# Weight loads, row statistics and three z blocks in a new order, from the last attention heads to loop iteration 12 of a fused layer

## The chip, the cores and the metric

One core of one Trainium2 chip runs the whole layer as one program. Times are device microseconds (us) of that core, from its first to its last instruction and the little that lies around them. TensorE (PE) multiplies, VectorE (DVE) and ScalarE (ACT) are the only engines besides PE that reach PSUM, GpSimd (POOL) works in SBUF alone, and SyncE (SP) issues almost every DMA.

## The reference

Four batches of 768 tokens (256 gathered image pixels projected to 192 channels, and 512 text rows) form `h`. Then, cut to what matters:

```
h = h + normed(attention(layernorm(h))) * silu(gate) @ Wo     # 6 heads, decay mask, group norm per batch
z = layernorm(h) @ P                                          # 8 sets of 16
scores = z . C (8 sets of 64);  top 4 of 64, softmax weights w
y = sum over the 4 chosen of w * (gelu(z @ W1 + b1) @ W2 + b2)
h = h + gelu(y @ G1 + g1b) @ G2 + g2b
```

The kernel computes all 64 experts of each set and multiplies by weights that are zero where an expert isn't chosen.

## The kernel before

There are 24 tiles of 128 tokens, handled as 12 pairs (k = 0 to 11) by the attention and as 6 blocks of 512 tokens by the experts. Each engine has its own instruction list, written out by hand, and the engines meet only at semaphores, so the order inside each list is the schedule.

**Attention.** The loop over pairs does queries, keys, values and gates of pair k and the heads, masks and outputs of pair k-1. `outputs` of pair 11 stands behind the loop: PE `turn` (transposed keys), `heads` (L590), DVE `mask`, PE `outputs` (L612, L615), DVE `outputs` (L1395), `group_stats` (L1403), `gn_aggr` (L1412). The group norm of the second half of the tokens needs all six pairs 6 to 11: PE `gn_mean`, DVE `gn_dev`, PE `gn_spread`, DVE `gn_var`, ACT `gn_root`, DVE `gn_scale`. Then DVE `normed` (L1462) scales pairs 6 to 8 and ACT `normed` (L1029) pairs 9 to 11, DVE `gate_mul` (L1447) multiplies by the gates, PE `wo_pair` (L643) projects, DVE `residual` adds into `h`.

**Preparation of the experts.** `row_stats` (L1474, L1475) takes the layer norm's statistics of a pair, `variances` (seven linked instructions, L1281 to L1287) and ACT `ln_root` and DVE `shifts` finish them for a range of tiles. `x2_make` normalises a pair (ACT before the loop, POOL at L1807 inside it), PE `turn_x2` transposes it, ACT `x2_out` copies it, PE `project_z` and ACT `z_out` give z of a block, and `z_high`, `z_rest`, `z_mid`, `z_low` split it in three bf16 parts that SP stores (`store_z`). For a tile of gates: `scores`, `copy_scores` (L1074), `largest` (L1504), `mark` (L1518), `distances`, `exps`, `chosen_exps` (L1535), `normaliser`, `weights` (L1784), `turn_gates` (L670), `keep_gates` (L1094), `high_part` and `low_parts`, `store_rows` and `store_gates`.

**The main loop.** It has 24 iterations i of 8 groups n. A group is: PE four `first` matmuls (L813), ACT three gelus (L1202, L1211, L1213), PE `duo_gates` (L852), DVE two products (L1668, L1671), POOL one (L1885), PE `second` (L876) two groups later. The weights of a group come by `spread`, an SP DMA of 512 KB (L368) issued three groups ahead into four buffers `wbc`. The gates of tile i+5 are made inside iteration i. Even iterations hold the exponentials of two tiles (n = 3, with two table loads on ACT), iterations 5, 9, ... the final projection of a block. Before the change z of blocks 3, 4 and 5 is made in iterations 1, 2 and 3, and their `x2_make` runs at n = 5 and 6 of iterations 0, 1 and 2. `load_w1` issues nine DMAs (six of 256 KB at L256, three of 16 KB at L260); half 0 goes on ACT's queue between two copies of pair 11, half 1 on SP's. `keep_clock(n)` issues n dummy matmuls of 512 columns (L760).

## Time and profile before

| what | before |
|---|---|
| median of 3 runs | 905.84 us (901.13 to 906.43) |
| the profiled execution's own time | 905.14 us |
| its span, first to last instruction | 903.3 us |
| granted TensorE clock, mean | 0.986 |
| first PE matmul of the main loop (L813) | 357.70 us |
| first DVE product of the main loop (L1668) | 359.44 us |

A profile page gives busy time by engine, the chain of work that ended last, and groups of instructions by line. The timeline lists instructions in order of time with the idle time before them and what released them. The windows view gives each engine's busy time in stretches that the reader chooses; below the stretches are loop iterations, from the first L1668 of one to the first L1668 of the next.

### The profile page before, as it was taken

What the parts mean: (1) busy time and instruction counts of PE and PEld (TensorE: products, weight loads), DVE (VectorE), ACT (ScalarE), POOL (GpSimd) and SP (SyncE); (2) the same over time, 40 slices, a digit from 0 to 9 for tenths busy, and PEclk for the clock granted to TensorE, in tenths of its full rate; (3) what the DMA queues carried; (4) which work ended last, traced back from release to release, by engine and by line L of the source; (5) the groups of instructions that cost most, each with busy time, mean ns of one, the idle gap of its engine ahead of it and who ended that gap; (6) DMA issues with size and microseconds to landing.
All of it is one profiled execution on the core that took longest, in us unless ns stands there. A gap on an engine that the chain in (4) does not pass through costs nothing.

```text
span 903.3 us, 16221 instructions
## 1 busy us (share of the span) xinstructions
PE 858.9 (95%) x5414; PEld 399.1 (44%) x5414; DVE 657.6 (73%) x1608; ACT 588.4 (65%) x891; POOL 527.9 (58%) x481
## 2 busy tenths in 40 slices
PE   8799999999999989889899999999999999999997
PEld 3477777777688756222222222322232223222222
DVE  5666656665476687958688888878888887877774
ACT  2232322345442356868689898889979897988784
POOL 0456555544365624566857576758675767575552
PEclk9999999999999999899999999999999999999998
DMA  9500002000000097768588989788988888989773
GB/s 266 221 1 1 2 1 75 1 1 1 1 2 13 18 156 176 241 190 260 170 262 236 277 233 289 235 282 235 282 236 277 252 275 230 280 257 301 250 247 102
DMA packets 90110, 154.28 MB, mean 171 GB/s; under 512 B 30326, under 2 KB 56374, under 8 KB 89635
## 3 DMA queue, kind: packets, MB, share of 16 engines
q1 hardware_dynamic: 89542, 151.63, 55.6%
q10 hardware_dynamic: 486, 1.62, 1.2%
q8 instruction: 44, 0.72, 0.3%
q14 instruction: 38, 0.31, 0.1%
HBM read 138.96 MB, written 15.83 MB: 171 GB/s over the span
## 4 chain that ended last, share of the span: by engine, by line
PE 75%; ACT 10%; DVE 7%; issue 4%; POOL 2%; DMA 1%; ACTq 0%; DVEq 0%; POOLq 0%; SPq 0%
PE ps L876 17%; PE ps L813 16%; PE ps L496 5%; PE ps L852 5%; PE ps L519 3%; PE ps L590 3%; PE ps L504 3%; PE ps L643 3%; PE ps L599 3%; ACT ring L1202 2%; PE ps L529 2%; PE ps L561 2%; PE ps L581 2%; PE ps L612 2%; PE ps L664 1%
## 5 line engine op out<-in xcount | busy, mean ns | idle before, releaser
L1885 POOL TENSOR_TENSOR ring<-ring,wbc 128x512 f32<-128x512 f32 x192 | 245.0, 1278 | 151.7 <-ACT ring L1211 142.3
L1668 DVE TENSOR_TENSOR ring<-ps,ring 128x1024 f32<-128x1024 f32 x192 | 234.6, 1222 | 82.3 <-PE ps L852 55.7
L813 PE MATMUL ps<-zst,w1st 99*128 99x512 bf16 x768 | 210.9, 384 | 12.3 <-ACT ring L1202 7.3
L876 PE MATMUL ps<-ring,w2cur 128*32 128x512 f32 x1536 | 206.6, 611 | 0.0
L1202 ACT ACTIVATE ring<-ps 128x1024 f32<-128x1024 f32 x192 | 196.9, 1026 | 3.9 <-PE ps L813 3.8
L1213 ACT ACTIVATE ps<-ps 128x512 f32<-128x512 f32 x192 | 113.3, 590 | 56.5 <-PE ps L813 56.3
L1671 DVE TENSOR_TENSOR ring<-ps,wbc 128x512 f32<-128x512 f32 x192 | 130.8, 681 | 0.2 <-DMA wbc<-w_rows 0.2
L813 PEld LDWEIGHTS ps<-zst,w1st 99*128 99x128 bf16 x768 | 60.7, 97 | 137.1 <-issue 37.3
L1211 ACT ACTIVATE ring<-ps 128x512 f32<-128x512 f32 x192 | 116.6, 607 | 0.0
L1734 POOL TENSOR_TENSOR s2q<-s2q,rope 128x768 f32<-128x768 f32 x24 | 43.1, 1817 | 91.0 <-ACT s2q L1014 91.0
L852 PEld LDWEIGHTS ps<-wst,sel 32*128 32x128 bf16 x384 | 18.1, 91 | 150.7 <-DVE ring L1668 95.9
L852 PE MATMUL ps<-wst,sel 32*128 32x512 bf16 x384 | 75.0, 387 | 4.9 <-DVE ring L1668 4.7
L1725 POOL TENSOR_TENSOR t1k<-t1k,t2k 128x768 f32<-128x768 f32 x24 | 44.1, 1853 | 52.8 <-DVE t2k L1351 52.8
L994 ACT COPY zT<-ps 128x512 f32<-128x512 f32 x12 | 7.0, 586 | 94.8 <-PE ps L489 94.8
L876 PEld LDWEIGHTS ps<-ring,w2cur 128*32 128x32 f32 x1536 | 31.9, 109 | 76.3 <-issue 70.4
L496 PE MATMUL ps<-wcat,zT 128*128 128x256 f32 (+2 forms) x144 | 53.8, 511 | 6.0 <-DVE t1q L1336 4.0
L1349 DVE TENSOR_TENSOR t1k<-ps,rope 128x768 f32<-128x768 f32 x24 | 22.9, 952 | 49.7 <-PE ps L599 41.1
L1336 DVE TENSOR_TENSOR t1q<-ps,rope 128x768 f32<-128x768 f32 x24 | 23.0, 957 | 46.9 <-PE ps L529 37.9
L1784 POOL TENSOR_TENSOR wn<-mr,norm 128x512 f32<-128x512 f32 x24 | 28.0, 1165 | 39.9 <-DVE mr L1535 36.7
L1743 POOL TENSOR_TENSOR qT<-t1q,s2q 128x768 f32<-128x768 f32 x24 | 43.2, 1823 | 0.0
L1518 DVE MATCH_REPLACE8 mr<-top,sc 128x68 f32<-128x68 f32 x192 | 39.0, 213 | 0.0
L1002 ACT COPY kT<-ps 128x768 f32<-128x768 f32 x24 | 19.1, 797 | 28.5 <-PE ps L581 28.5
(181 smaller groups left out, 1297.7 us busy)
## 6 DMA issues: line engine op xcount, KB each, us to landing
wbc<-w_rows SPq DMA_DIRECT2D x192, 512.0 KB, 5.3
w2cur<-in_w SPq DMA_DIRECT2D x48, 256.0 KB, 4.9
w_parts<-wp SPq DMA_DIRECT2D x72, 64.0 KB, 3.1
zst<-z_parts SPq DMA_DIRECT2D x72, 64.0 KB, 4.3
wst<-w_parts SPq DMA_DIRECT2D x24, 128.0 KB, 4.0
z_parts<-zp SPq DMA_DIRECT2D x6, 384.0 KB, 6.3
wst<-w_parts SPq DMA_DIRECT2D x24, 96.0 KB, 3.8
out_h<-h SPq DMA_DIRECT2D x12, 192.0 KB, 5.4
```

The costliest lines, as they stand in the source:

```text
L496: pe.matmul(bank(to + a // 512, 0, w), xnT[:, k % 2, x, :], wcat[:, 0, col + a:col + a + w], start=True, stop=False)
L813: return pe.matmul(bank(to), w1st[0:99, 4 * a + j, col:col + P], zst[0:99, (i // 2) % 2, j, :], start=True, stop=True)
L852: mm = pe.matmul(bank(WBANK + j), sel[q:q + 32, n % 2, :], wst[q:q + 32, i % 2, j, :], start=True, stop=True)
L876: mm = pe.matmul(bank(YBANK, 0, 512, 32 * j, 32 * j + 32), w2cur[:, n, j, :], ring[:, (4 * g + j) % RING, :], start=False, stop=(n == 7 an ...
L1202: act.activation(ring[:, slot:slot + 2, :].rearrange("p a n -> p (a n)"), ps[:, 0:2 * BLK], ACT.Gelu_apprx_tanh).then_inc(s["duo_gelu"], 1)
L1211: act.activation(ring[:, slot + 3, :], bank(TBANK), ACT.Gelu_apprx_tanh).then_inc(s["tri_gelu"], 1)
L1213: act.activation(bank(JBANK), bank(JBANK), ACT.Gelu_apprx_tanh).then_inc(s["two_gelu"], 1)
L1668: dve.tensor_tensor(v, ps[:, WBANK * 512:WBANK * 512 + 1024], v, ALU.mult).then_inc(s["duo_done"], 1)
L1671: dve.tensor_tensor(ring[:, slot + 2, :], bank(JBANK), wbc[:, g % 4, 0, :], ALU.mult).then_inc(s["two_done"], 1)
L1725: pool.tensor_tensor(v, v, t2k[:, x, :, :].rearrange("p h d -> p (h d)"), ALU.add).then_inc(s["ak"], 1)
L1743: pool.tensor_tensor(qT[:, x, :, :].rearrange("p h n -> p (h n)"), t1q[:, x, :, :].rearrange("p h n -> p (h n)"), s2q[:, x, :, :].rearrang ...
L1885: pool.tensor_tensor(ring[:, slot, :], ring[:, slot, :], wbc[:, g % 4, 1, :], ALU.mult).then_inc(s["tri_done"], 1)
```

## The change

- **Weights.** `load_w1(0)` moves from ACT's queue to SP's, behind `store_z(0)`; `load_w1(1)` moves from before the end of attention to the last place ahead of the loop's first `spread` calls, behind `load_z(0)` and `load_gates(0)`. The first three spreads go ahead of these. The ones of `zst` are loaded in two halves. The loads of G1, g1b, G2 move into iteration 1 (semaphore `ld_final`) and that of g2b into iteration 2; `store_z(1)` and `store_z(2)` into iteration 0.
- **Statistics.** `mark(2)` and `row_stats(2)` to `(4)` go into pair 11 ahead of `rotate_keys`, `row_stats(5)` and `variances(4, 12)` to its end. `row_stats(6)` to `(9)` go to iteration 0 (n = 3), `row_stats(10)`, `(11)`, `variances(12, 24)` and `ln_root(5)` to iteration 2 (n = 3), `shifts(5)` to its n = 4.
- **Before the loop.** Heads of pair 11 ahead of `turn_gates(2)`; PE `outputs` waits for its own half's mask alone; `group_stats` by half; `chosen_exps(3)` ahead of the masks; `turn_gates(3)` ahead of the group norm; `project_z(1)` ahead of `gn_spread`; DVE `normed` in two calls (pair 6, then 7 and 8); `largest(5)` and the first part of `mark(5)` ahead of the loop. `keep_clock` goes from nine dummy matmuls to two.
- **z of blocks 3 to 5** is made in iterations 4, 8 and 12, and its `x2_make` on POOL in iterations 3, 7 and 11, one tile in each of n = 2 to 5.

```diff
+            load_w1(sp, 0)
+            store_rows(2)
+            store_rows(3)
+            store_gates(2)
+            store_gates(3)
             sp.wait_ge(s["aq"], TILES)
             sp.wait_ge(s["ak"], TILES)
-            load_w1(sp, 1)
...
+            for g in range(3):
+                spread(g)
+            sp.wait_ge(s["yg_t"], 2)
+            load_ones(0)
             sp.wait_ge(s["st_z"], 16)
             load_z(0)
+            sp.wait_ge(s["yg_t"], 4)
             sp.wait_ge(s["zeroed"], 16)
             load_gates(0)
+            load_ones(1)
+            load_w1(sp, 1)
...
-                pe.wait_ge(s["m"], 2 * k + 2)
+                pe.wait_ge(s["m"], 2 * k + x + 1)
...
+            heads(PAIRS - 1, 0)
+            heads(PAIRS - 1, 1)
             turn_gates(2, 1)
             pe.wait_ge(s["res"], 6)
-            keep_clock(2)
-            heads(PAIRS - 1, 0)
-            heads(PAIRS - 1, 1)
-            keep_clock(2)
+            keep_clock(1)
             outputs(PAIRS - 1, 0)
             outputs(PAIRS - 1, 1)
+            pe.wait_ge(s["wT_done"], 3)
+            turn_gates(3, 1)
...
-            keep_clock(2)
+            keep_clock(1)
             gn_mean(1, 6)
-            pe.wait_ge(s["x2_e"], 4)
+            project_z(1, 7)
             turn_x2(4, 2)
             gn_spread(1, 6)
             turn_x2(5, 3)
...
-                if i in (1, 2, 3):
-                    if n == 0 and i == 2:
+                if i in (4, 8, 12):
+                    later = i // 4 + 2
+                    if n == 0:
                         pe.wait_ge(s["wT_done"], tile - 1)
-                        turn_x2(2 * i + 4, PBANK)
+                        pe.wait_ge(s["s_copied"], tile + 1)
+                        turn_x2(2 * later, PBANK)
...
             keep(PAIRS - 1, 0)
-            load_w1(act, 0)
             copy_scores(3, 0)
             keep(PAIRS - 1, 1)
...
-                if g == 2:
+                if i == 0 and n == 3:
+                    for k in range(6, 10):
+                        row_stats(k)
+                if i == 2 and n == 3:
                     row_stats(10)
                     row_stats(11)
                     dve.wait_ge(s["st2"], PAIRS)
                     variances(12, 24)
...
-                if i < 3 and n in (5, 6):
-                    x2_make(2 * i + 1 + n)
+                if i in (3, 7, 11) and 2 <= n < 6:
+                    x2_make(i // 4 * 2 + 6 + (n - 2) // 2, n % 2)
```

## Rows read from the trace of the kernel before

**Rows 1.** The page's first section: engine, busy us, share of the span, instructions.

```profile
PE 858.9 (95%) x5414; PEld 399.1 (44%) x5414; DVE 657.6 (73%) x1608; ACT 588.4 (65%) x891; POOL 527.9 (58%) x481
```

**Rows 2.** Windows: iterations 0, 1, 2, 4 and 7, busy time by engine, granted clock, DMA.

```profile
359.44:389.53 30.09, 24.22 (x114) 6.34 (x115) 24.18 (x80) 23.16 (x34) 19.74 (x21) 0.83 0.67 224
389.53:413.44 23.91, 23.20 (x130) 6.62 (x129) 18.24 (x45) 19.12 (x33) 16.99 (x18) 1.00 0.79 234
413.44:443.87 30.43, 25.81 (x142) 7.55 (x141) 20.30 (x53) 24.31 (x38) 20.62 (x22) 0.94 0.69 206
...
467.72:490.15 22.43, 21.45 (x130) 5.90 (x129) 18.93 (x51) 21.43 (x31) 15.28 (x15) 1.00 0.87 259
...
535.00:554.38 19.38, 19.38 (x116) 4.98 (x115) 17.02 (x44) 16.61 (x26) 15.25 (x18) 1.00 0.83 258
```

**Rows 3.** Timeline of DVE, L1668 around the last group of iteration 2.

```profile
436.90 1.22 DVE L1668 TENSOR_TENSOR ring<-ps,ring 128x1024 f32<-128x1024 f32 x1
...
443.87 1.23 DVE L1668 TENSOR_TENSOR ring<-ps,ring 128x1024 f32<-128x1024 f32 x1 [4.54 <-PE ps L852]
```

**Rows 4.** The same, the last group of iteration 4, which ends at 490.15.

```profile
487.59 1.23 DVE L1668 TENSOR_TENSOR ring<-ps,ring 128x1024 f32<-128x1024 f32 x1
```

**Rows 5.** Timeline of ACT after pair 11; ACTq is its DMA issue.

```profile
316.80 3.15 ACTq L256 DMA_DIRECT2D w1st<-w_parts  x6
...
321.70 0.81 ACT L1002 COPY kT<-ps 128x768 f32<-128x768 f32 x1
```

**Rows 6.** The chain that ended last, 316 to 358 us: start, us, what.

```profile
322.56 2.96 PE ps L590 x24
...
341.10 6.23 PE ps L643 x36
...
349.24 6.05 PE ps L643 x36
355.29 1.72 PE ps L760 x4
```

**Rows 7.** Timeline of DVE, group norm of the second half.

```profile
332.20 1.20 DVE L1412 BATCH_NORM_AGGREGATE gmv<-gns 128x2 f32<-128x36 f32 x6
...
337.28 2.78 DVE L1462 TENSOR_SCALAR oT_b<-oT_b,gscale,gbias 128x384 f32<-128x384 f32 x6
340.09 2.69 DVE L1447 TENSOR_TENSOR oT_b<-oT_b,gate_b 128x768 f32<-128x768 f32 x3
```

**Rows 8.** Timeline of DVE, statistics in iteration 0: the first of four, the seven links' ends.

```profile
367.55 0.34 DVE L1474 BATCH_NORM_STATS2 stats<-h 128x6 f32<-128x192 f32 x1
...
368.70 1.24 DVE L1281 TENSOR_TENSOR lns<-stats 128x12 f32<-128x12 f32 x1
...
371.03 0.17 DVE L1287 SCALAR_TENSOR_TENSOR lns<-lns 128x12 f32<-128x12 f32 x1
```

**Rows 9.** Timeline of DVE, iteration 4, n = 3: the wait for the exponentials.

```profile
477.69 0.69 DVE L1535 SCALAR_TENSOR_TENSOR mr<-mr,dist 128x512 f32<-128x512 f32 x1 [1.64 <-ACT dist L1087]
```

**Rows 10.** Timeline of ACT, iteration 4, n = 3: the table load back to gelu.

```profile
477.61 1.28 ACT L1202 ACT_TABLE_LOAD   x1
```

**Rows 11.** Timeline of POOL, iteration 2, n = 6: normalising ahead of `weights`.

```profile
437.12 1.99 POOL L1807 TENSOR_SCALAR x<-h,mean,rstd 128x192 f32<-128x192 f32 x2
```

**Rows 12.** Timeline of PE, the same place.

```profile
440.26 1.09 PE L670 MATMUL ps<-ident,wn 128*128 128x128 f32 x4 [2.75 <-POOL wn L1784]
```

**Rows 13.** Timeline of SP's queue: `load_w1(1)` and the next issue.

```profile
328.49 6.02 SPq L256 DMA_DIRECT2D w1st<-w_parts  x6
...
335.61 0.36 SPq L394 DMA_DIRECT2D sel<-in_sel  x1
```

**Rows 14.** DMA, 334 to 344 us: queue, packets, MB, share; KB, us to landing.

```profile
q1 hardware_dynamic: 1125, 1.58, 106.4%
...
sel<-in_sel SPq DMA_DIRECT2D x1, 64.0 KB, 11.6
```

**Rows 15.** Windows: a stretch of iteration 0 at the low clock (columns as in rows 2).

```profile
365.00:372.00 7.00, 6.84 (x25) 1.29 (x25) 6.76 (x19) 5.48 (x8) 2.65 (x3) 0.51 0.82 277
```

More of the change, by code:

```diff
@@ L427, in _ @@
                     store_out(i // 4 - 1)
-                if n == 6 and i in (1, 2, 3):
-                    store_z(i + 2)
+                if n in (1, 2) and i == 0:
+                    store_z(n)
+                if n >= 3 and i == 1:
+                    dst, src = finals[n - 3]
+                    sp.dma_start(dst, src).then_inc(s["ld_final"], 16)
+                if n == 0 and i == 2:
+                    sp.dma_start(g2b[:, :], t["g2"][GH:GH + 1, :].to_broadcast([P, D])).then_inc(s["ld_bias"], 16)
+                if n == 6 and i in (4, 8, 12):
+                    store_z(i // 4 + 2)
                 if n == 6 and i + 1 < NIT:
@@ L785, in _ @@
             scores(4, 0)
-            keep_clock(1)
+            project_z(2, 7)
             wo_pair(6, 4)
             wo_pair(7, 5)
-            pe.wait_ge(s["x2_e"], 6)
             wo_pair(8, 2)
-            project_z(2, 7)
-            wo_pair(9, 3)
+            pe.wait_ge(s["z_e"], 3)
+            scores(LEAD, PBANK)
+            pe.wait_ge(s["wT_done"], 4)
+            wo_pair(9, 1)
             pe.wait_ge(s["res"], 7)
@@ L1451, in gate_mul, with normed @@
                     ins.then_inc(s["yg_t"], 1)
-            def normed(half):
+            def normed(k0, k1):
                 bb = 1
@@ L1567, in _ @@
                     largest(2, 0, S)
+                    mark(2, 0, S)
+                    row_stats(2)
+                    row_stats(3)
+                    row_stats(4)
                 rotate_keys(k, 0)
@@ L1614, in _ @@
                     normaliser(2)
-            for c in range(2, 6):
-                row_stats(c)
-            dve.wait_ge(s["st2"], 6)
-            variances(4, 12)
+                    row_stats(5)
+                    dve.wait_ge(s["st2"], 6)
+                    variances(4, 12)
             largest(3, 0, S)
             mark(3, 0, S)
+            chosen_exps(3)
             mask(PAIRS - 1, 0)
+            shifts(4, 4, 12)
             mask(PAIRS - 1, 1)
-            shifts(4, 4, 12)
+            normaliser(3)
             outputs(PAIRS - 1, 0)
+            group_stats(PAIRS - 1, 0)
             outputs(PAIRS - 1, 1)
-            group_stats(PAIRS - 1)
+            group_stats(PAIRS - 1, 1)
             gn_aggr(1)
-            chosen_exps(3)
-            normaliser(3)
             gn_dev(1, 6)
@@ L1638, in _ @@
             largest(4, 0, S)
+            gate_mul(9)
+            mark(4, 0, S)
             residual(6, 4)
-            gate_mul(9)
             gate_mul(10)
@@ L1644, in _ @@
             residual(8, 2)
-            mark(4, 0, S)
-            residual(9, 3)
-            row_stats(6)
+            largest(LEAD, 0, S)
+            residual(9, 1)
             residual(10, 4)
-            row_stats(7)
             residual(11, 5)
-            row_stats(8)
-            row_stats(9)
+            mark(LEAD, 0, 3)
             def finish(blk, half, at):
@@ L1683, in _ @@
                     variances(12, 24)
-                if g == 4:
+                if i == 2 and n == 4:
                     shifts(5, 12, 24)
                 if n in (0, 1) and tile < TILES:
-                    if i == 0 and n == 0:
-                        largest(tile, 0, S)
-                        mark(tile, 0, 3)
                     mark(tile, 3 * n + 3, min(S, 3 * n + 6))
```

126 lines of the change are left out of this document (56 added, 70 removed).

## The prediction

> **What bounds the kernel.** I read the page's engine list first: PE is busy 95% of the span [rows 1], so no engine off PE's path matters by its total, and what can be won are stalls and PE's own filler. Then I cut the main loop into iterations with the windows [rows 2]. The reader is to see three lengths: 22.43 us for an undisturbed even iteration (4), 19.38 for an odd one without a final projection (7), and 30.09, 23.91 and 30.43 for iterations 0, 1 and 2; iteration 3 repeats 1 with 23.85. In iteration 7 PE is busy all of the time. In an even one ACT and PE are both near 21.4 of 22.43. So the excess of the first four iterations over their undisturbed kind, 7.7 + 4.5 + 8.0 + 4.5 = 24.7 us, is what the moved work costs today. Last I read the chain between pair 11 and the loop [rows 6] with the timelines beside it.
>
> **Start of the loop, a gain of 7.7 us.** I follow PE's chain. (a) ACT issues nine weight DMAs between the first and the second copy of kT; the first six take 3.15 us, and the second copy starts at 321.70 [rows 5], after which the heads run at 322.56 [rows 6]. Without them PE's transposes of the second half set it: they end about 318.5, the copy takes 0.81, heads start near 319.4, 3.1 earlier. (b) Heads take 2.96. Each output needs its own mask alone, and the statistics of half 0 go under the outputs of half 1: another 1.1 together, so aggregation (1.20, now to 333.4 [rows 7]) ends near 329.2, 4.2 earlier. For that DVE must be free: `mark(2)` and three `row_stats` go into its wait ahead of `rotate_keys` of pair 11, which is longer than they are, and `chosen_exps(3)`, ahead of the masks, is done as the heads end. Cover gone, the latter costs 0.9 on the path. (c) `project_z(1)` ahead of `gn_spread` delays the group norm by 1.0, less 0.4 for the exponentials moved away: its scale is ready at 333.6 rather than 337.2. (d) `normed` for three pairs takes 2.78 [rows 7]; for pair 6 alone about 1.15 (a third of the elements plus the fixed part; with the second call 0.4 more in all), then one `gate_mul`, 0.9. PE could start `wo_pair(6)` at 335.7, but its own scores(4) and z of block 2 come first: 336.5, 4.6 ahead of 341.10 [rows 6]. (e) From there PE is the chain. Before: two runs of three `wo_pair` (6.23 and 6.05), 1.9 of z between, 1.72 of dummies [rows 6] and 0.86 of scores, 16.6 in all. After: 12.4 + 0.95 = 13.4. The first L813 starts at 350.0, not 357.70. DVE's list, laid out with the same durations, has the last residual at 350.5 and its first L1668 at 351.7, not 359.44. The bounds are 5 us if each of some ten semaphore hops slips by 0.3, 8.7 if the norm's wait behind `project_z` is absorbed. I take 7.7, which comes from the durations themselves.
>
> **Iteration 0, a gain of 6.3.** Out go `largest(5)` and part of `mark(5)` (counted above), statistics of two pairs, the seven `variances` links (368.70 to 371.2 [rows 8]), the sqrt tables and two `x2_make`. What is left is iteration 4's pattern, 22.4, with eight `row_stats` instructions at n = 3, 0.26 to 0.3 each (first of its kind in [rows 8]), 2.1 in sum. DVE waits 1.64 there for the exponentials [rows 9], so 0.4 stays: 22.8, 7.3 less than 30.09. The clock adds to this: a stall of the first groups behind `largest(5)` left PE short of work, and the next 7 us ran at 0.51 [rows 15]; with the cause out, I count no low stretch. Against it stands SP's queue. `load_w1(1)` is issued from about 343.8, behind the gates of tile group 0, and `spread(3)` comes behind it. Its six large issues took 6.02 [rows 13]; with the three small ones, spread 3 is issued near 350.8, its data behind 1.6 MB. Group 3 asks for it at 351.7 + 6.5 + 1.1 = 359.4. Between 334 and 344 us only 1.58 MB moved although the engines were fully busy [rows 14], so the weights take 11 us: to 355 or 356, and spread 3 lands at 358 to 360. The nearest harder row is the DMA right behind this same batch: issued at 335.61, landed 11.6 later [rows 13, 14], 18.7 after the batch began; so priced, spread 3 lands at 364.5, 5.1 late. The range is 0 to 5; that row had the other half's data still in the engines, so I take 1.0. The other SP moves (G1, G2, g2b, z stores 1 and 2) are single issues of about 0.4 in front of spreads that are three groups ahead, and their users are in iterations 4 and 5: nothing. The wait of `load_z(0)` on two gate products holds back the gates and weights alone, since the first three spreads are ahead of it.
>
> **Iterations 1, 2 and 3, gains of 4.5, 6.0 and 4.4.** Iteration 1 becomes a plain odd one, 23.91 to 19.4 [rows 2]; the finals are SP issues only. Iteration 3 becomes 19.4 from 23.85, less 0.1: its four `x2_make` halves on POOL are 1.0 each (half of 1.99 [rows 11]), beside a product of 1.28 in a group of 2.3, and `second` asks for POOL's product two groups later. Cover gone, all twelve would cost up to 12 us in three iterations; POOL is idle a fifth of an odd iteration [rows 2], so I count 0.1 here and nothing later. Iteration 2 loses z (3.6) and the stall of its last group. That group takes 443.87 - 436.90 = 6.97 [rows 3] against 490.15 - 487.59 = 2.56 in iteration 4 [rows 2, 4]: POOL spends 1.99 on `x2_make` ahead of `weights` [rows 11], PE's transposes wait 2.75 for it [rows 12], and the rest of the group queues behind. It gains 4.4. Iteration 2 also receives at n = 3 two pairs' statistics (1.1), `variances` (2.5 [rows 8], first link slow beside a POOL instruction) and on ACT the square root with one more table load, 1.28 [rows 10] + 0.2. DVE absorbs 1.64 [rows 9]; both sides leave 1.5 to 2.0, more if both contend, up to 3. I take 2.0. 30.43 - 3.6 - 4.4 + 2.0 = 24.4.
>
> **Iterations 4, 8 and 12, a loss of 10.8.** Iteration 2 of before is the same pattern at the same n, so its first seven groups price it: 436.90 - 413.44 = 23.46, against 487.59 - 467.72 = 19.87 in iteration 4 [rows 2 to 4]; 3.6 each. Bounds: 2.9, which is ACT's extra busy time (24.31 - 21.43), and 4.5, which is iteration 1's excess. POOL's new `add_bias` neighbours are in iteration 4 already.
>
> **Sum.** -7.7 - 6.3 - 4.5 - 6.0 - 4.4 + 10.8 = -18.1. Against the profiled execution, 905.14, that is 887; the median of the three runs is 905.84, near enough that I don't correct.
>
> **Rivals.** *A, the weights in front of the spreads.* The batch drains as slowly as in [rows 13, 14]; groups 3 and after wait for `wbc`, which delays 5.1 instead of 1.0: 891 to 892. For it: the full DMA engines behind that batch. Against: half of that time went to the other batch. The Trainium skill, "DMA: Bandwidth & Descriptors", section "Queues, rings and completion order", says that descriptors of one queue are consumed in ring order while different queues take turns. By that rule the stores and spreads now queue behind all of the weights on SP's ring, where ACT's queue used to alternate with them, and the time is this rival's.
> *B, the clock, on the other side.* Seven of nine dummies are gone. If PE falls to the lower level, 1.2 GHz, at its first wait after the heads (near 324) and stays there up to the loop, its 22 us of work from heads to the last `wo_pair` take up to as much again: the loop starts at 372, and the sum turns to +4: 909. It decides against the change once more than 18 us of PE work runs at half speed. For it: PE did run at 0.51 after a stall [rows 15], and iteration 2, with its wait of 2.75 [rows 12], shows a mean of 0.94 [rows 2]. Against: my layout has no PE wait above 1.2 us ahead of the loop, and the first matmul of the loop is reached with PE busy nearly all of the last 14 us. The same skill, "TensorE: Matmul & The Clock Gate", section "HAM oscillation", ties such drops to recurring idle gaps; by the gaps that I find it would not act here.
> *C, the norm's chain keeps its length.* The heads gain 3.1, but the order of DVE and ACT lists (exponentials ahead of masks, two table loads, x2 copies ahead of `gn_root`) returns what (b) to (d) win: start gain 3.1 only, 891.7. For it: seven engine changes in a row there. Against: each list has idle time at that point.
>
> **Chances.** Forecast 0.58 (883 to 890), A 0.20 (890 to 895), C 0.10, better than 883 with z cheaper in the even iterations 0.05, B with its partial forms 0.07. The range of 881 to 896 takes in the bounds of the start (5 to 8.7), of z (8.7 to 13.5 for the three) and of the weights (0 to 5), and leaves out B. Within 1% (about what a measurement of this kernel can tell from no change) means above 896.8: faster 0.88, same 0.08, slower 0.04, the last when B and A meet.
>
> **What would show it.** In the changed profile: first L1668 at 351 to 353; iterations 0 to 3 of 23 to 24, 19.4, 24.4 and 19.5; 4, 8 and 12 of 26, and 16 and later unchanged. A shows as DVE or POOL waiting on wbc at groups 3 to 6. B shows as a granted clock near 0.5 between 324 and 352. C shows as heads near 319.4 with the first L813 after 353. I am wrong if PE's stalls simply reappear in the even iterations at n = 3 to 5, where ACT is full.

## The result, and the profile after

| what | before | after |
|---|---|---|
| median (13 runs each, same chip) | 905.43 us | 896.94 us (893.08 to 901.68) |
| ratio after / before, 95% interval | | 0.9908 [0.989, 0.9927] |
| the profiled execution's own time | 905.14 us | 900.31 us |
| last xnT copy of the attention loop (pair 11) | 285.49 | 288.07 |
| from there to the first product of the loop | 73.95 | 75.57 |
| first to last product of the loop | 531.54 | 522.61 |

The change gains 8.5 us, not 18. The marks in this table are starts in the two traces. The xnT copy is ACT's copy of the normalised tokens at the head of a pair (L994 in before; the rows name its tile zT). The profiled execution of after is 2.58 us late before the changed code begins: pair 11's xnT copy comes at 288.07 instead of 285.49, and pair 1's was already as late (44.24 instead of 41.66) in code that both kernels share. In all these executions pair 1's copy stands between 39.59 and 44.28, in the same code, so kernels are compared here from pair 11's copy on: 73.95 + 531.54 = 605.49 before, 75.57 + 522.61 = 598.18 after, 7.3 less. In the rows of after L820 is the kernel before's L813, L859 its L852, L883 its L876, L1679 and L1682 its L1668 and L1671, L1897 its L1885, L655 its L643, L602 its L590.

The page's first section of after, to be read against [rows 1]:

```profile
PE 854.4 (95%) x5400; PEld 398.0 (44%) x5400; DVE 657.9 (73%) x1614; ACT 589.0 (66%) x891; POOL 527.8 (59%) x481
```

Nothing in the totals tells the difference, as nothing in them told what could be won. Windows of after, iterations 0 to 4 and 7 (columns as in [rows 2]: length, PE, PEld, DVE, ACT, POOL, granted clock, DMA share, GB/s):

```profile
363.64:387.61 23.97, 23.97 (x115) 6.59 (x115) 21.01 (x57) 22.09 (x32) 14.95 (x15) 0.78 0.98 270
387.61:408.02 20.41, 19.50 (x117) 4.98 (x116) 17.11 (x43) 16.65 (x27) 13.91 (x16) 1.00 0.90 256
408.02:433.34 25.32, 22.82 (x130) 5.99 (x129) 21.42 (x64) 23.03 (x33) 15.05 (x16) 0.93 0.82 241
433.34:452.71 19.37, 19.37 (x117) 5.08 (x116) 17.01 (x43) 16.61 (x26) 19.05 (x23) 1.00 0.89 253
452.71:478.71 26.00, 24.13 (x142) 7.33 (x141) 20.30 (x52) 24.23 (x38) 15.67 (x16) 1.00 0.80 243
523.57:542.94 19.37, 19.37 (x117) 5.08 (x116) 17.01 (x43) 16.61 (x26) 19.11 (x23) 1.00 0.88 277
```

The loop did nearly what was forecast. Iterations 0 to 3 fell by 6.1, 3.5, 5.1 and 4.5; 4, 8 and 12 rose from 22.43 to 26.0 each. The DMA share of iteration 0 is 0.98 where it was 0.67: the first sign of what follows. PE is busy in all of iteration 0, at a mean granted clock of 0.78; that comes back below. Now the stretch that answers to [rows 6]. The timeline of PE, after:

```profile
322.05 2.94 PE L602 MATMUL ps<-qT,kT 128*128 128x128 f32 x24 [0.89 <-ACT kT L1009]
...
340.49 2.22 PE L655 MATMUL ps<-wo,oT_b 128*128 128x192 f32 x12
344.33 4.17 PE L655 MATMUL ps<-wo,oT_b 128*128 128x192 f32 x24 [1.62 <-DVE oT_b L1456]
...
349.19 6.27 PE L655 MATMUL ps<-wo,oT_b 128*128 128x192 f32 x36
361.54 1.01 PE L820 MATMUL ps<-zst,w1st 99*128 99x512 bf16 x2 [6.07 <-DMA zst<-in_ones]
```

PE's own work ahead of the loop ends near 355.4, 67.4 after the last copy; before it ended at 357.0, 71.5 after the copy. Then PE stands for 6.07 us until a DMA of 12 KB has landed, and the gain of the start is gone. SP's queue shows what stood around that DMA (start, duration of the issues, line, count):

```profile
321.01 2.92 SPq L256 DMA_DIRECT2D w1st<-w_parts  x6
...
333.01 10.89 SPq L327 DMA_DIRECT2D w_parts<-wp  x6
...
346.29 1.87 SPq L368 DMA_DIRECT2D wbc<-w_rows  x3
348.20 0.47 SPq L386 DMA_DIRECT2D zst<-in_ones  x1
348.78 3.80 SPq L338 DMA_DIRECT2D zst<-z_parts  x6
...
354.04 0.30 SPq L386 DMA_DIRECT2D zst<-in_ones  x1
354.39 3.85 SPq L256 DMA_DIRECT2D w1st<-w_parts  x6
...
359.21 7.01 SPq L368 DMA_DIRECT2D wbc<-w_rows  x2
```

Ahead of the ones stand the first three spreads (1.5 MB), behind them the second half of w1 (1.6 MB, here called the batch). Windows of after and then of before, 10 us each, show the DMA engines (last two columns):

```profile
340.00:350.00 10.00, 8.38 (x45) 7.12 (x44) 9.89 (x38) 6.10 (x12) 7.71 (x9) 1.00 0.44 128
350.00:360.00 10.00, 5.44 (x33) 4.88 (x31) 6.62 (x25) 1.01 (x2) 1.52 (x2) 1.00 1.03 241
360.00:370.00 10.00, 8.46 (x23) 1.98 (x23) 6.22 (x16) 6.63 (x10) 4.82 (x5) 0.53 1.05 163
370.00:380.00 10.00, 10.00 (x51) 2.37 (x51) 7.76 (x20) 9.52 (x13) 4.10 (x5) 0.79 1.05 333
```

```profile
330.00:340.00 10.00, 8.25 (x41) 4.30 (x38) 8.63 (x31) 4.79 (x12) 1.04 (x1) 1.00 1.06 171
340.00:350.00 10.00, 9.87 (x48) 7.39 (x47) 9.16 (x20) 6.37 (x15) 5.99 (x7) 1.00 0.75 152
350.00:360.00 10.00, 9.69 (x48) 6.64 (x46) 6.23 (x30) 4.72 (x8) 3.35 (x5) 1.00 0.64 190
360.00:370.00 10.00, 6.65 (x25) 1.63 (x28) 9.81 (x39) 7.26 (x11) 6.21 (x6) 0.76 0.90 308
370.00:380.00 10.00, 9.78 (x57) 2.46 (x49) 8.70 (x24) 9.93 (x15) 4.14 (x4) 0.90 0.59 185
```

After, the engines are at their limit from 350 to 380, just where PE needs its first data; before, they had been full from 330 to 340, while PE needed nothing, and had room in each of the next four windows. A share of 1.05 with only 163 GB/s (360 to 370, while the batch moves) and the same share with 333 GB/s (370 to 380, the spreads) say that a byte of the batch is about twice as dear.

### The profile page after: what moved, and what is told of

Read it like the earlier page. It is cut to its first block, busy times and chain, and to the rows that moved or that the text cites. A ratio compares the mean times of both kernels' runs of the same rounds, so it can differ in the third digit from the quotient of the medians.

```text
span 898.5 us, 16202 instructions
## 1 busy us (share of the span) xinstructions
PE 854.4 (95%) x5400; PEld 398.0 (44%) x5400; DVE 657.9 (73%) x1614; ACT 589.0 (66%) x891; POOL 527.8 (59%) x481
## 4 chain that ended last, share of the span: by engine, by line
PE 79%; ACT 10%; DVE 6%; issue 2%; DMA 2%; POOL 0%; SPq 0%; DVEq 0%; POOLq 0%; ACTq 0%
PE ps L883 18%; PE ps L820 18%; PE ps L508 6%; PE ps L859 6%; PE ps L531 3%; PE ps L516 3%; PE ps L602 3%; PE ps L611 3%; PE ps L541 2%; PE ps L593 2%; ACT ring L1210 2%; PE ps L573 2%; PE ps L624 2%; PE ps L655 1%; PE ps L676 1%
## 5 line engine op out<-in xcount | busy, mean ns | idle before, releaser
L1897 POOL TENSOR_TENSOR ring<-ring,wbc 128x512 f32<-128x512 f32 x192 | 245.1, 1278 | 151.0 <-ACT ring L1219 142.5
L1679 DVE TENSOR_TENSOR ring<-ps,ring 128x1024 f32<-128x1024 f32 x192 | 234.7, 1222 | 79.9 <-PE ps L859 51.5
L820 PE MATMUL ps<-zst,w1st 99*128 99x512 bf16 x768 | 212.9, 388 | 20.6 <-ACT ring L1210 10.7
L883 PE MATMUL ps<-ring,w2cur 128*32 128x512 f32 x1536 | 205.5, 608 | 0.0
L1682 DVE TENSOR_TENSOR ring<-ps,wbc 128x512 f32<-128x512 f32 x192 | 130.9, 682 | 1.4 <-DMA wbc<-w_rows 1.3
L820 PEld LDWEIGHTS ps<-zst,w1st 99*128 99x128 bf16 x768 | 61.3, 98 | 141.9 <-issue 42.9
L859 PEld LDWEIGHTS ps<-wst,sel 32*128 32x128 bf16 x384 | 18.1, 91 | 149.3 <-DVE ring L1679 92.7
L859 PE MATMUL ps<-wst,sel 32*128 32x512 bf16 x384 | 75.6, 390 | 1.5 <-DVE ring L1679 1.3
L883 PEld LDWEIGHTS ps<-ring,w2cur 128*32 128x32 f32 x1536 | 31.7, 108 | 77.4 <-issue 69.8
L508 PE MATMUL ps<-wcat,zT 128*128 128x256 f32 (+2 forms) x144 | 55.9, 528 | 4.9 <-DVE t1q L1345 2.9
```

The lines of the kernel that those rows point to most:

```text
L508: pe.matmul(bank(to + a // 512, 0, w), xnT[:, k % 2, x, :], wcat[:, 0, col + a:col + a + w], start=True, stop=False)
L820: return pe.matmul(bank(to), w1st[0:99, 4 * a + j, col:col + P], zst[0:99, (i // 2) % 2, j, :], start=True, stop=True)
L859: mm = pe.matmul(bank(WBANK + j), sel[q:q + 32, n % 2, :], wst[q:q + 32, i % 2, j, :], start=True, stop=True)
L883: mm = pe.matmul(bank(YBANK, 0, 512, 32 * j, 32 * j + 32), w2cur[:, n, j, :], ring[:, (4 * g + j) % RING, :], start=False, stop=(n == 7 an ...
L1679: dve.tensor_tensor(v, ps[:, WBANK * 512:WBANK * 512 + 1024], v, ALU.mult).then_inc(s["duo_done"], 1)
L1682: dve.tensor_tensor(ring[:, slot + 2, :], bank(JBANK), wbc[:, g % 4, 0, :], ALU.mult).then_inc(s["two_done"], 1)
```

## The experiments

All ratios are to the kernel before on the same chip. "Start" is the time from the last xnT copy to the first product of the loop, "loop" from first to last product. All eighteen kernels are told, in the order of the questions.

**1. The wait for the ones (e1, e2, e3).** My first reading was that a shared semaphore makes PE wait for ones that only group 16 needs.

```diff
-t["ones"][:, 1024 * m:1024 * m + 1024]).then_inc(s["ld_late"], 16)
+t["ones"][:, 1024 * m:1024 * m + 1024]).then_inc(s["ld_ones1" if m else "ld_late"], 16)
-            pe.wait_ge(s["ld_late"], 16 * 3)
+            pe.wait_ge(s["ld_late"], 16 * 2)
+                    pe.wait_ge(s["ld_ones1"], 16)
```

> The changed kernel, with the second half of the ones counted on a semaphore of its own and awaited at group 16, its first user, and not ahead of group 0. Theory 1 (the wait for this small load is what holds the start of the loop): PE idles under 1 us instead of 6.07 between the last wo_pair and the first L820-type matmul, the stretch at the low clock behind it is gone or shorter, and the ratio to the kernel before is 0.983 to 0.985, 5 to 7 us better than the changed kernel. Rival (the first z parts or gates land as late, and the wait only changes its name): the idle time stays above 4 us and the ratio stays at 0.990.

Measured: 897.71 us, 0.9905 [0.987, 0.994], start 74.08, loop 527.04. The wait changed its name (timeline of PE, e1):

```profile
359.42 0.59 PE L820 MATMUL ps<-zst,w1st 99*128 99x512 bf16 x2 [3.93 <-DMA zst<-z_parts]
361.45 0.61 PE L860 MATMUL ps<-wst,sel 32*128 32x512 bf16 x2 [1.44 <-DMA wst<-w_parts]
```

The z parts and the gates are just as late. That theory fell: the ones, the z parts and the gates are all late. The next kernel sends the batch into the loop, one of its nine pieces behind each spread of groups 3 to 11; e3 has both edits.

```diff
-            load_w1(sp, 1)
+                if 3 <= g < 12:
+                    load_w1(sp, 1, (g - 3,))
```

> The changed kernel, with the nine loads of weight half 1 issued one per group in groups 3 to 11 instead of in one batch ahead of the loop; the wait for the ones stays. Theory 1 (the ones land 7.1 us after their issue because 1.6 MB of weights share the DMA engines behind them): they land within 3 us, PE idles 1.5 to 2.5 us, ratio 0.984 to 0.987. Rival (they land late because of what is in front of them, z parts and gates): landing stays above 6 us and the ratio near 0.990. Spreads of groups 4 to 12 have one more issue in front of each; if DMA is the limit there, DVE waits on wbc in iterations 0 and 1, 1 to 2 us.

> Both edits together. If the semaphore alone removes the wait (theory 1 of the first run), this adds only what the weights cost the first spreads: 0 to 1.5 us more, ratio 0.981 to 0.985. If the spreads were late behind the weights (rival A of the prediction), the first four groups get 3 to 5 us shorter than in the first run, ratio below 0.981.

Measured: e2 903.64 us, 0.9976 [0.9955, 0.9996], start 72.68, loop 529.90; e3 904.43 us, 0.9984 [0.9963, 1.0006], start 71.83, loop 529.84. Against after, the start gains 2.9 and 3.7, and the loop loses 7: iteration 1 takes 27.48 us in e2, with DVE waiting for `wbc` in five groups (up to 3.2). None of the expected ratios came: the loop had been expected to pay 2 us at most. The work went to another place and was paid there.

**2. The loop's part alone (e4).** The kernel before with z of blocks 3 to 5 in iterations 4, 8 and 12 and `x2_make` in 3, 7 and 11, nothing else.

```diff
-                if i in (1, 2, 3):
+                if i in (4, 8, 12):
-                if i < 3 and n in (5, 6):
-                    x2_make(2 * i + 1 + n)
+                if i in (3, 7, 11) and 2 <= n < 6:
+                    x2_make(i // 4 * 2 + 6 + (n - 2) // 2, n % 2)
```

> The kernel before with one part of the change alone: z of blocks 3 to 5 in iterations 4, 8 and 12, its x2_make on POOL in 3, 7 and 11. By the prediction's sum: iteration 0 gains 3.8 (no x2_make ahead of the gates), 1 gains 4.5, 2 gains 8.0, 3 gains 4.4, and 4, 8 and 12 lose 3.6 each: 9.9 us, ratio 0.989. Rival (the stalls come back in the even iterations, which have no room): under 4 us, ratio above 0.995.

Measured: 896.21 us, 0.9902 [0.9865, 0.9939], start 73.95, loop 525.45. The forecast for this part held (0.989), and it is worth as much as the whole change, within the intervals. Iterations 0 to 4 take 26.29, 23.04, 23.30, 19.38 and 26.01; iteration 0 lost the stall of its last group, iteration 1 has one wait for `wbc` of 3.06. So all that was done ahead of the loop and to the statistics returns nothing, net, within the intervals: in the traces after's loop is 2.8 shorter than e4's and its start 1.6 longer.

**3. The batch elsewhere on the queue (e5 to e8).** The diff is e5's. In e6 and e7 the batch stands right behind `load_w1(sp, 0)`, e7 with e1's edit besides; e8 leaves the batch and puts half 0 back on ACT's queue.

```diff
             store_gates(2)
+            load_w1(sp, 1)
             store_gates(3)
...
-            load_w1(sp, 1)
```

> The changed kernel with one move undone: weight half 1 is issued behind the gates of tile 2, about where it stood in the kernel before, not in front of the loop; half 0 stays on SP's queue. Theory 1 (the 1.6 MB of weight half 1, slow to drain, was hidden ahead of the loop and now stands in its way): the ones and z parts land within 4 us, PE idles under 2 us ahead of the loop instead of 6.07, landing of spreads in the first 50 us of the loop falls from 7 to 8 us to near 5, no waits on wbc; 6 to 8 us better than the changed kernel, ratio 0.982 to 0.985. Rival (DMA work before the loop is the same in any order, so the start is as late): ratio 0.988 to 0.991.

> The changed kernel with both weight halves back to back on SP's queue as soon as attention's weights are free, ahead of the rows and gates of tiles 2 and 3. Theory 1: the DMA engines are full from 321 to 343 and free afterwards, the loop starts earliest of all orders, ratio 0.980 to 0.985. Rival: the stores of gates 2 land after 343, POOL's high part of tile 3 and with it the gates of block 0 come late, and PE waits for wst as long as it waits now: ratio 0.988 or more.

> As the run before, and the second half of the ones on its own semaphore. If the ones land quickly once the weights are out of the way (theory 1), this changes nothing beyond 1 us. If they are slow by themselves, it gains 2 to 4 us over the run before.

> The changed kernel with the other move undone: weight half 0 is issued on ACT's queue again, half 1 stays in front of the loop. By the prediction (part a) the heads of pair 11 start 3 us later, and so does what follows, ratio 0.993 to 0.994 against 0.991 of the changed kernel. If DMA sets the start of the loop (theory 1), the 3 us are hidden behind its wait of 6.07 and the ratio stays at 0.990 to 0.992.

Measured: e5 899.48 us, 0.9934 [0.9908, 0.9959], start 78.18, loop 521.16. e6 908.23 us, 1.0028 [1.0009, 1.0046], start 87.78. e7 908.72 us, 1.0019 [0.9995, 1.0044], start 86.56. e8 896.10 us, 0.9883 [0.9851, 0.9916], start 74.34, loop 521.72. The loop is clean in e5 as its theory said (iterations 1 and 2 take 19.38 and 23.98), the start is not. With nothing of w1 behind the ones, e5 has PE waiting for them still longer than after, 8.66 us; so "the weights behind the ones" fell too as the whole cause: what stands *in front* holds them. In e5 that is the spreads and, as part 4 shows, the batch, by way of a store. e6 is what its rival said, and e7 adds nothing clear of the intervals to it. In e6 both halves are in front of the small stores of gates 2, and POOL, which may not overwrite their buffer, stands (timeline of POOL, e6):

```profile
349.69 0.40 POOL L1802 CAST wp<-wT_even 128x256 bf16<-128x256 f32 x1 [21.50 <-DMA w_parts<-wp]
```

In after the same wait is 6.72, and in e8, with half 0 on ACT's queue, 3.65. That is the rule of the Trainium skill, "DMA: Bandwidth & Descriptors", section "Queues, rings and completion order": a queue's descriptors go in its ring's order, while queues take turns. The three waits agree with it. The total came out the same in e8 as in after, within the intervals, as the second expectation had it. The heads of pair 11 start 37.16 after the xnT copy instead of 33.98, so the 3.2 us of part (a) of the prediction are real on PE's list, and yet the start is 1.2 earlier: PE's list did not set it.

**4. Who goes first (e9, e10, e11).** In e9 the first three spreads go behind the gates and ones, the batch stays last. e10 also has the batch behind the store of gates 2; e11 besides has half 0 on ACT's queue.

```diff
-            for g in range(3):
-                spread(g)
             sp.wait_ge(s["yg_t"], 2)
...
             load_ones(1)
+            for g in range(3):
+                spread(g)
             load_w1(sp, 1)
```

> The changed kernel with the first three spreads issued behind the z parts, the gates of block 0 and the ones, as in the kernel before, and weight half 1 still last. Theory 2 (1.5 MB of spreads in front of 0.6 MB that PE needs first hold the loop): the ones land within 3 us, PE idles under 2 us instead of 6.07, the first product of the loop stands 4 to 5 us earlier, measured from the last xnT copy; spread 0 is now awaited by group 0, 0 to 2 us. Iterations 1 and 2 still pay 2.4 us for weight half 1. Ratio 0.985 to 0.988. Rival (the DMA engines are full up to 362 whatever the order): the start stays and the ratio stays at 0.990.

> As the run before, and weight half 1 issued behind the gates of tile 2. If both orders matter, the loop is clean from iteration 1 (19.4 and 24.0, seen with this place of the weights) and the start is no later than in the run before: ratio 0.981 to 0.985. If the batch pushes the gates' stores and z parts back by its 11 us, as it seems to have done with the spreads in front, the start is 2 to 4 us later than in the run before and the ratio 0.986 to 0.990.

> As the run before, with weight half 0 back on ACT's queue. The rows and gates of tiles 2 and 3 are no longer behind it on SP's ring, POOL's wait for the store of gates 2 falls from 6.7 to under 4, but the heads of pair 11 are 3 us later. If DMA sets the start, ratio equal to or up to 2 us below the run before. If PE's chain does, 2 to 3 us above it.

Measured: e9 898.23 us, 0.9933 [0.9909, 0.9958], start 68.87, loop 529.27. e10 893.03 us, 0.9872 [0.9845, 0.9898], start 72.83, loop 521.25. e11 896.23 us, 0.9893 [0.9865, 0.9921], start 76.02, loop 522.19. In e9 PE waits for no DMA at all, and for the first time its own chain is seen bare: 68.87, a gain of 5.1 on before. It is all given back in iteration 0, which takes 32.98 (timeline of DVE, e9):

```profile
373.01 0.69 DVE L1682 TENSOR_TENSOR ring<-ps,wbc 128x512 f32<-128x512 f32 x1 [10.42 <-DMA wbc<-w_rows]
```

The fourth group's weights stand behind the batch, and the expected ratio of 0.985 to 0.988 did not come. e10 has the lowest median of the kernels with all the work in them, 4 us under after's (3.3 by the ratios, whose intervals just meet); it came as its second expectation said. The batch in front, where the engines were half idle, costs PE 3.74 us for the ones and nothing that shows in iterations 0 and 1 (23.5 and 19.37).

How it costs that is seen on SP's queue. `load_gates(0)` waits until `store_gates(3)` has landed, and in e10 this store stands behind the batch. Its last piece (issue view, e10) and the gates' load (queue) are:

```profile
w_parts<-wp SPq DMA_DIRECT2D x1, 64.0 KB, 11.8
...
352.42 0.34 SPq L349 DMA_DIRECT2D wst<-w_parts  x1
```

The same two in e9, with all three pieces of the store:

```profile
w_parts<-wp SPq DMA_DIRECT2D x3, 64.0 KB, 1.7
...
346.48 0.36 SPq L349 DMA_DIRECT2D wst<-w_parts  x1
```

So the load of the gates goes out 67.2 us after the xnT copy in e10 and 61.0 in e9, and the second half of the ones goes out behind it. e11, whose order of batch, small loads and spreads is nearly that of before, has the same wait: POOL's wait falls to 3.83 as expected, but its gates go out at 70.3, PE waits 3.01 for the ones, and the start is the latest of the three. In e5 the gates go out at 66.4, in after at 64.6.

**5. Less at a time, and a shorter chain (e12, e13, e14).** e12 is after with `normed(6, 8)` in one call. e13 is e9 with four pieces of the batch behind the store of gates 2 and five behind that of gates 3, and nothing of it behind the spreads; e14 is both. (Where the expectations say blocks 0 to 2 and pairs 6 and 7, the edits move the spreads of groups 0 to 2 and norm pairs 6 to 8.)

```diff
+            load_w1(sp, 1, range(4))
             store_gates(3)
+            load_w1(sp, 1, range(4, 9))
```

> The changed kernel with DVE's normed for pairs 6 to 8 in one call, as before (undoes one part of step d). In the changed kernel the two calls take 1.63 + 3.09 us, against 2.78 in one call before, and PE waits 1.62 for the second gate product. If splitting costs (fixed parts, and POOL's high part beside it), one call takes 2.8 to 3.5 and the last wo_pair ends up to 1 us earlier. As PE waits 6.07 for DMA behind it, the time doesn't change in either case: ratio 0.990 to 0.992.

> The changed kernel with the spreads of blocks 0 to 2 behind the gates of block 0 and the vector of ones, and with the second half of w1 in two parts: four pieces behind the store of gates 2, five behind the store of gates 3. Theory (the DMA engines' time ahead of the loop is the limit, and with the spreads behind the small loads the engines stood idle in two stretches of 10 us, 330 to 350): the pieces of the first part fall into the idle stretches and those of the second are half a batch only, so PE waits under 2 us for the ones or z parts, the first product of the loop comes 69 to 71 us after the last xnT copy, the loop takes 521 to 523 us, and the ratio to the kernel before is 0.982 to 0.986 (about 890 us). Rival (anything of w1 ahead of the small loads holds them by the same latency): PE still waits 3.5 us or more, start at 72 to 73, ratio 0.987.

> As e13_w1_split, and the oT of pairs 6 and 7 are normed in one call instead of two. Theory: with PE's own chain setting the start, the shorter chain of VectorE shows as 1 us less than e13_w1_split, ratio 0.981 to 0.985. Rival (the DMAs still set the start): no difference from e13_w1_split, since the wait grows by what the chain gains.

Measured: e12 896.48 us, 0.9901 [0.9868, 0.9935], start 74.51, PE's wait 5.75. e13 895.39 us, 0.9899 [0.9872, 0.9926], start 74.5, loop 520.85, PE's wait 5.18. e14 896.99 us, 0.9919 [0.989, 0.9949], start 75.48, PE's wait 7.1. My theory of e13 missed: the DMA engines are then full without a break from 320 to 360 (shares 1.08, 0.97, 1.09, 0.95 in its 10-us windows), the idle stretches are filled, and there is still not enough time. In e12 and e14 PE's last `wo_pair` ends 0.75 and 1.2 us earlier after the xnT copy than in after and e13. The start does not follow it: 1.1 earlier in e12, 1.0 later in e14. So e14's rival held in the main, and one start that hangs on a DMA is known to about 1 us; three starts of before's order (before, e4, e18) lie within 0.13.

**6. The batch alone, moved and left out (e15 to e18).** e15 is the kernel before with nothing changed but the batch's place: behind the first three spreads, as in after.

```diff
-            load_w1(sp, 1)
...
             for g in range(3):
                 spread(g)
+            load_w1(sp, 1)
```

> The kernel before with the second half of w1 alone moved, to just behind the first three spreads ahead of the loop. Theory (the batch takes some 11 us of all DMA engines, and costs nothing in the kernel before only because it drains in a stretch in which the engines are idle): the loop's first spreads land late, iterations 0 and 1 grow by 5 to 10 us together, ratio to the kernel before 1.005 to 1.011. Rival (the batch isn't what the changed kernel waits for): ratio 0.998 to 1.002.

Measured: 910.91 us, 1.0078 [1.0051, 1.0105], start 74.18, loop 538.59. Iteration 0 takes 36.59 instead of 30.09, and the waits of 357 to 395 us in e15 hold two that before has none of there:

```profile
POOL ring L1885 <- DMA wbc<-w_rows: 13.8, 1, 13.8
...
DVE ring L1671 <- DMA wbc<-w_rows: 8.9, 1, 8.9
```

So the late batch costs 5.4 us by the medians (910.91 against 905.52; 6.5 in iteration 0), in an order that is otherwise the old one. The last three leave the batch's six large pieces out; the slots of the second half are computed with the first half's weights, with the same instructions.

```diff
             for n, k in enumerate((0, 1, 0, 2, 0, 1)):
+                if a:
+                    continue
-w1st[0:99, 4 * a + j, col:col + P]
+w1st[0:99, j, col:col + P]
```

> The changed kernel with the six large pieces of the second half of w1 (1.5 MB) left out, nothing else moved; the slots of the second half are computed with the weights of the first, so the output differs in those columns, and the instructions of all engines are the same. Theory (the batch's 11 us of DMA time are what the start and the late spreads cost): PE waits under 2.5 us for the ones or z parts instead of 6.07, the first product of the loop comes 69 to 72 us after the last xnT copy instead of 75.57, the loop takes 520.5 to 521.5 instead of 522.61, ratio to the kernel before 0.981 to 0.986. Rival (PE's own chain or the clock sets the start): start 74 or later, ratio 0.988 to 0.991.

> As e16_no_w1b, with the first three spreads behind the gates of block 0 and the vector of ones (the edit of e9_spreads_behind_gates). Theory: start at 68.9 as in e9_spreads_behind_gates, and iteration 0 without its gap of 16.15 us: 22.5 to 23.5, loop 520.5 to 521.5, ratio 0.980 to 0.983, the predicted 887 or near it. Rival: the spreads are late in any case, since they are issued where they are needed: iteration 0 above 26, ratio 0.985 or more.

> The kernel before with the same six pieces left out. Theory (there the batch drains in a stretch in which the engines would be idle): nothing to gain, ratio 0.998 to 1.001. Rival (the batch costs the kernel before as much as the changed one, so that it can't be what separates them): ratio 0.990 to 0.995.

Measured: e16 894.94 us, 0.9885 [0.9864, 0.9907], start 73.84, loop 521.33. e17 893.90 us, 0.9858 [0.9831, 0.9886], start 68.93, loop 522.54. e18 905.88 us, 1.0004 [0.9991, 1.0017], start 73.83, loop 531.44. The kernel before pays nothing for the batch, under 0.1% by the interval. Windows of e18, to be read against the same two of before above:

```profile
330.00:340.00 10.00, 8.25 (x41) 4.30 (x37) 8.66 (x31) 4.81 (x12) 1.04 (x1) 1.00 0.51 131
340.00:350.00 10.00, 9.87 (x48) 7.38 (x47) 9.16 (x20) 6.37 (x15) 6.01 (x7) 1.00 0.17 35
```

The shares fall by 0.55 and 0.58, so the batch is 11.3 us of all DMA engines, and before it lay in time that nobody else wanted. e16's theory missed: without the batch the start gains 1.7 only, because the three spreads in front still hold the ones. Its numbers are near those of the rival, but what PE waits for is a DMA and not its own chain (timeline of PE, e16):

```profile
355.30 1.01 PE L822 MATMUL ps<-zst,w1st 99*128 99x512 bf16 x2 [4.28 <-DMA zst<-in_ones]
```

e17 moves these too, and the wait is gone (timeline of PE, e17):

```profile
349.25 6.27 PE L657 MATMUL ps<-wo,oT_b 128*128 128x192 f32 x36
355.36 0.60 PE L822 MATMUL ps<-zst,w1st 99*128 99x512 bf16 x2
```

Start 68.93 and iteration 0 at 23.72 stand together only here. e17's start came as expected; its ratio did not (0.980 to 0.983 was expected), nor did its loop. So moving the spreads behind the small loads gives 6.7 us of the start with the batch there (75.57 - 68.87, e9) and 4.9 without it (73.84 - 68.93, e17 against e16), and leaving out the batch alone gives 1.7. And the batch takes 9.3 of iteration 0 once the start is early (32.98 in e9, 23.72 in e17). In every order tried with all the work in it, one of the two came late.

## Why the prediction was wrong

The direction was right, but the size falls just short of "faster by over 1%", which was given 0.88: the ratio is 0.991, and "same" had been given 0.08. The time missed the range of 881 to 896 by 0.9 us. From the last xnT copy on, the forecast was 18.1 less and 7.3 came: 10.8 short.

**The step that failed is "Start of the loop, a gain of 7.7 us".** The start came out 1.6 us later than before, 9.3 short. The runs split this in two, each part known to about 1 us.

- *Part (e), "From there PE is the chain": 6.6 us short, shown by e9 and e17.* I laid out PE's, DVE's and ACT's lists and never SP's: not when the ones, z parts and gates would land, only when the spreads would. The three moved spreads were costed as nothing because their own users aren't hurt; but the small loads behind them are. In before the gates went out at 353.1 to 354.0 with the spreads behind, and landed in 2.0 to 2.2 us; in after they took 4.4, 5.9 and 7.6. For the batch I had "the weights take 11 us" from [rows 14], which is right (11.3), and didn't ask what else needs the engines in the same 40 us.
- *The same gap, in the term for spread 3.* The batch was to be issued at 343.8 and spread 3 to land at 358 to 360. Less the offset of 2.58, the batch went out at 351.8 and POOL had spread 3 at 369.8, 10 us behind the 359.4 at which the forecast asks for it; the range was 0 to 5. In e9, where the start is early, this is the wait of 10.42. In after it hides behind the late start (timeline of POOL, after):

```profile
372.37 1.28 POOL L1897 TENSOR_TENSOR ring<-ring,wbc 128x512 f32<-128x512 f32 x1 [2.21 <-DMA wbc<-w_rows]
```

  The harder price in the prediction, 364.5, doesn't follow from its rows either: 350.8 + 11.6 and 343.8 + 18.7 are 362.4 and 362.5, 3 us late and not 5.1.
- *Parts (b) to (d): 2.7 us too much, seen in e9 and e17 (68.87 and 68.93; 66.25 was forecast).* Allowing for the offset of 2.58, the heads stand at 322.05 where 322.0 was forecast, so part (a) is right to 0.1, and e8, which undoes it, has them 3.2 later. Aggregation ends at 333.05, 1.25 late; the group norm's scale stands at 337.65, 1.45 late; the first `wo_pair` at 340.49, 1.4 late. The second stands another 1.62 for `oT_b`. The timeline of DVE, after:

```profile
326.04 0.69 DVE L1543 SCALAR_TENSOR_TENSOR mr<-mr,dist 128x512 f32<-128x512 f32 x1 [0.56 <-ACT dist L1085]
326.65 0.95 DVE L1396 TENSOR_TENSOR pT<-ps,causal 128x768 f32<-128x768 f32 x1
...
331.85 1.20 DVE L1421 BATCH_NORM_AGGREGATE gmv<-gns 128x2 f32<-128x36 f32 x6
...
337.65 1.63 DVE L1470 TENSOR_SCALAR oT_b<-oT_b,gscale,gbias 128x128 f32<-128x128 f32 x6
339.31 0.96 DVE L1456 TENSOR_TENSOR oT_b<-oT_b,gate_b 128x768 f32<-128x768 f32 x1
340.19 3.09 DVE L1470 TENSOR_SCALAR oT_b<-oT_b,gscale,gbias 128x256 f32<-128x256 f32 x6
```

  The mask starts 1.7 after the heads' end (324.99) because `chosen_exps(3)` sits in front of it and its exponentials end late; the cover that I named for it isn't there. And `normed` in two calls is 1.63 + 3.09 = 4.7 against 2.78 in one [rows 7]; I had counted 1.15 for the first and 0.4 for the split. The second call is that long because POOL works beside it; in e6, where POOL stands for its store until 349.69, it isn't (timeline of DVE, e6):

```profile
335.78 2.02 DVE L1470 TENSOR_SCALAR oT_b<-oT_b,gscale,gbias 128x256 f32<-128x256 f32 x6
```

  In after POOL is there because it waited 6.72 for the store behind w1's half 0, and came into DVE's way at 339.31. e7, where POOL stands as well, has 2.02 too. e12 takes the split back, and PE's last `wo_pair` ends 0.75 earlier.

**The rest of the sum held, in part by luck.** Iteration 0: 23.8 forecast, 23.97 measured, out of two terms that were wrong. The 1.0 for the late spreads cost nothing that shows, since the late start hid them. "I count no low stretch" was wrong: PE ran at 0.50 behind the wait (windows of after, under the rivals) and was busy in all of the iteration, where the pattern taken from iteration 4 has PE busy 21.45 of 22.43. Iteration 0 of e13 and of e6 (windows) shows it with the DMA engines a quarter idle: PE is again busy in all of it, and the length goes with the granted clock.

```profile
360.01:384.60 24.59, 24.59 (x115) 6.67 (x115) 21.05 (x57) 22.18 (x32) 14.97 (x15) 0.76 0.73 220
371.43:394.62 23.19, 23.19 (x115) 6.51 (x115) 21.05 (x58) 21.93 (x32) 14.95 (x15) 0.81 0.76 231
```

Iteration 1: 19.4, measured 20.41; the late weights reach it, with DVE waiting 0.94 for `wbc` at 406.81. It is 19.4 in e5, e8, e10, e13, e16 and e17, but in e12 too, which has after's DMA order, so this 1.0 doesn't come in every execution. Iteration 2: 24.4, measured 25.32. In the kernels with the changed statistics it takes 24.0, or 25.3 and more, and the granted clock tells which: 1.00 in the six with 24.0 (e3, e5, e8, e9, e12, e13), 0.93 or less in all others. The group at n = 3 takes 7.25 in each of them; the two groups behind it are longer where the clock fell. Iteration 2 of e9 (windows), to be read against after's above:

```profile
406.66:430.63 23.97, 21.45 (x130) 5.92 (x129) 21.43 (x63) 22.97 (x33) 13.79 (x14) 1.00 0.87 262
```

So iteration 2 held but for 1.4 us of clock, and why the clock falls there in one kernel's trace and not in another's stays open. Iteration 3: 19.5, measured 19.37. Iterations 4, 8 and 12: +3.6 each, measured 26.0 - 22.43 = 3.6. The loop as a whole was forecast 10.4 shorter and is 8.9. e4 shows that moving z is right by itself.

**The rivals.** A named the cause, full DMA engines and ring order, and its sign is there (POOL waits 2.21 and 1.18 for `wbc` in groups 3 and 5), but it went wrong in who pays: it charged the spreads of iteration 0 with 5.1, in place of the small loads that PE waits for ahead of it. Its time, 891 to 892, is also too low, since it kept the start's 7.7. B did not come as told. PE did not fall at 324: the granted clock is 1.00 up to 360. The low stretch came behind the wait (windows of after):

```profile
355.00:360.00 5.00, 0.46 (x3) 0.17 (x2) 1.69 (x10) 0.00 (x0) 0.00 (x0) 1.00 1.11 191
360.00:365.00 5.00, 3.46 (x9) 0.74 (x9) 1.36 (x2) 2.17 (x4) 0.67 (x1) 0.56 1.04 158
365.00:370.00 5.00, 5.00 (x15) 1.25 (x14) 4.86 (x15) 4.46 (x7) 4.16 (x5) 0.50 1.05 167
```

  0.50 is the lower level, 1.2 GHz. The first three groups take 2.36 each there, against 2.32, 2.12 and 2.07 in iteration 4 of before, 0.6 in all; the iteration as a whole is told above. e17 has such a stretch as well, 0.57 in 360 to 365, without a long wait, and before has 0.52 in 365 to 370, so a low stretch there is not new with the change. C's price of a norm chain that keeps its length would be 4.6; 2.7 of that came.

**What stays open.** e10 still waits 3.74 for the ones, and e17, which leaves work out, is only 0.14% faster by its ratio, within the intervals. The whole batch behind the store of gates 3 and ahead of the small loads was not tried. Whether an order with all the work reaches a start of 69 and an iteration 0 of 23.7 was not shown; e13 says that filling the idle stretches isn't enough. An earlier start of the batch than e6's, at 320.53, was not tried, since its place in SBUF is in use by attention until then.

## What to carry to other kernels

When a change moves DMAs, lay out the queue and the DMA engines' time like an engine's list: for each load that the bound engine waits for, sum what is in front of it on its queue, and price it by the share it takes, not by its bytes. A batch that costs nothing where it is may be paying with idle time that the new place doesn't have; a kernel with that one batch moved (e15) and one with it left out (e18) tell that in two runs. And when a gain ahead of a loop vanishes, look for the first wait on a DMA behind it before blaming the chain: removing one wait (e1) renames it, and shortening the chain (e14) lengthens it. A load can also wait for a store: look at what stands in front of that too (e10).

## What the hardware showed that was not expected

- 1.5 MB in six DMAs to 16 partitions each take 11.3 us of all 16 engines (e18 against before), some 140 GB/s; the spreads, to 128 partitions, run at 333 GB/s at the same share (370 to 380 in after). A byte of the one costs some 2.3 times a byte of the other. The two differ in their sources too (the spreads read each row many times), and no run parts that from the number of partitions.
- A DMA of 12 KB took 7.14 us (354.04 to 361.18 in after), for what stood in its queue and not for its size: in e10 the same DMA goes out at 353.74, and PE starts at 356.33.
- DVE and POOL slow each other on SBUF: six 128x256 TENSOR_SCALAR take 3.09 beside POOL (after) and 2.02 without (e6), while POOL's 128x256 cast at 339.31, beside DVE's gate product, takes 1.22 where another one at 341.34 takes 0.40. And a third of the elements is not a third of the time: six of 128x128 take 1.63, six of 128x384 take 2.78.
- The same instructions of iteration 2 run at a mean granted clock of 1.00 in 23.97 us (e9) or at 0.93 in 25.32 (after); the two kernels differ only in the place of three spreads ahead of the loop.
- The same code ahead of pair 1 took up to 4.7 us more in one execution than in another (xnT copies of pair 1 at 39.59 to 44.28): compare from a mark behind it.
